# Gated heads: the value experts' columns laid out with the expert innermost

## The reference

```python
gates = sigmoid((x @ w_gate).reshape(b, n, HEADS, EXPERTS).transpose(0, 2, 1, 3))
sel = argmax(gates, axis=-1)
gm = one_hot(sel, EXPERTS) * gates
values = einsum('bhne,ehdk,bnd->bhnk', gm, value_experts, x)
sim = einsum('bhid,bhjd->bhij', q * SCALE, k)        # causal mask, then softmax
out = einsum('bhij,bhjk->bhik', attn, values)
out = einsum('bhne,ehkd,bhnk->bhnd', gm, output_experts, out)
return out.sum(axis=1)
```

## Time and profile before

| what | value |
|---|---|
| runs, us | 4002.11, 4003.85, 4009.77 (median 4003.85) |
| profiled execution, us | 4002.22 |
| its span, us | 4000.5 |
| mean granted TensorE clock | 0.958 |
| TensorE matmul busy | 3622.6 us (91%) |
| TensorE weight load busy | 3018.5 us (75%) |
| VectorE busy | 2943.7 us (74%) |
| ScalarE busy | 2167.8 us (54%) |
| stage `gated_heads` | about 2808 to 4000 us |

### The profile page before, as it was taken

One profiled execution on the slowest core, in us unless ns is written; L12 is line 12 of the kernel. 1 busy time (PEld: TensorE's weight loads), 2 busy tenths in 40 slices (PEclk: granted clock), 3 DMA queues, 4 the chain that ended last, 5 costly groups with the idle time before them and its releaser, 6 DMA issues. The chain is left out here.

```text
span 4000.5 us, 93426 instructions
## 1 busy us (share of the span) xinstructions
PE 3622.6 (91%) x28994; PEld 3018.5 (75%) x28994; DVE 2943.7 (74%) x9189; ACT 2167.8 (54%) x6661; POOL 300.2 (8%) x382
## 2 busy tenths in 40 slices
PE   6999999899999998079877879998799999999998
PEld 5888888688888887069755656666588888888887
DVE  5666666677777775556567768888888888888886
ACT  5777777677777774135344447777333333333333
POOL 0000000000000000521286000000000000000000
PEclk9999999899999997589989889999899999999999
DMA  2000000100000002422211000000200000000000
GB/s 97 0 0 0 0 0 0 47 24 10 10 10 10 16 6 101 132 94 78 71 48 31 0 19 21 16 21 16 93 14 11 13 10 13 8 10 13 10 11 9
DMA packets 56112, 109.74 MB, mean 27 GB/s; under 512 B 8368, under 2 KB 27184, under 8 KB 55728
## 3 DMA queue, kind: packets, MB, share of 16 engines
q1 hardware_dynamic: 46656, 80.72, 6.3%
q0 software_dynamic: 8464, 26.22, 2.0%
q10 hardware_dynamic: 864, 1.19, 0.1%
HBM read 72.46 MB, written 35.65 MB: 27 GB/s over the span
## 5 line engine op out<-in xcount | busy, mean ns | idle before, releaser
L639 ACT ACTIVATE c_pr<-c_sm,c_nmx 128x256 f32<-128x256 f32 x512 | 254.5, 499 | 153.6 <-DVE c_nmx L485 153.6
L127 PE MATMUL f_ps_out<-f_out_rounded,f_zgT 128*128 128x256 f32 x1024 | 310.4, 303 | 0.0
L128 PE MATMUL f_ps_out<-f_out_rest,f_zgT 128*128 128x256 f32 x1024 | 288.7, 282 | 0.0
L129 PE MATMUL f_ps_out<-f_out_rounded,f_zgT 128*128 128x256 f32 x1024 | 286.5, 280 | 0.0
L639 ACT ACTIVATE a_pr<-a_sm,a_nmx 128x128 f32<-128x128 f32 (+1 forms) x512 | 227.3, 445 | 106.0 <-DVE a_nmx L485 105.9
L485 DVE CUSTOM_DVE_ANT_0 a_sm<-a_ps_s,causal 128x128 f32<-128x128 f32 (+1 forms) x512 | 152.6, 355 | 164.2 <-PE a_ps_s L371 164.2
L2151 DVE TENSOR_REDUCE f_v<-f_gv 128x64 f32<-128x512 f32 x256 | 268.6, 1049 | 0.4
L1742 ACT ACTIVATE c_pr<-c_ps_s,c_nmx 128x256 f32<-128x256 f32 x512 | 213.8, 499 | 88.9 <-DVE c_nmx L1574 88.9
L485 DVE CUSTOM_DVE_ANT_0 c_sm<-c_ps_s,c_mask 128x256 f32<-128x256 f32 x512 | 186.8, 421 | 92.0 <-PE c_ps_s L371 90.2
L2301 ACT CAST f_zgT<-f_ps_g 128x512 fp32r<-128x512 f32 x256 | 151.3, 591 | 184.4 <-PE f_ps_g L2031 184.4
L2142 DVE TENSOR_TENSOR f_gv<-f_ps_v,f_gm_step 128x512 f32<-128x512 f32 x256 | 175.2, 684 | 98.1 <-PE f_ps_v L129 86.6
(11 more groups left out here) (377 smaller groups left out, 11442.2 us busy)
## 6 DMA issues: line engine op xcount, KB each, us to landing
f_slot_rows<-f_run POOLq DMA_DIRECT2D x1, 9216.0 KB, 34.9
f_rows<-f_slot_rows SPq DMA_DIRECT2D x72, 128.0 KB, 2.0
f_slot_out<-f_y SPq DMA_DIRECT2D x72, 128.0 KB, 1.9
c_ctx_stage<-in_ctxT SPq DMA_DIRECT2D x32, 256.0 KB, 2.8
small<-in_f_w SPq DMA_DIRECT2D x16, 512.0 KB, 3.9
x_sb<-in_x SPq DMA_DIRECT2D x8, 512.0 KB, 7.9
small<-in_c_w SPq DMA_DIRECT2D x8, 512.0 KB, 3.8
c_mask_stage<-in_mask SPq DMA_DIRECT2D x16, 256.0 KB, 3.0
```

What stands on the lines that cost most here:

```text
L127: nc.tensor.matmul(out, sh, mh, start=start, stop=False, **kw)
L128: nc.tensor.matmul(out, sh, ml, start=False, stop=False, **kw)
L129: return nc.tensor.matmul(out, sl, mh, start=False, stop=stop, **kw)
L639: last = nc.scalar.activation(pr[:, r, i, 0:n], sm[:, j, i, 0:n], ACT.Exp, bias=nmx[:, j, i:i + 1], scale=-1.0, accum_out=sums[:, r, i:i + 1])
```

## The change

The columns of `f1_val` are laid out as (channel, expert): column k*8 + e. The gating reads PSUM and writes `gv` in that order, with the eight gates broadcast along the channels, and the sum reads eight adjacent words. The sum adds the same eight terms in the same order of experts. Sizes, counts, waits and the order of the work stay.

```diff
-        gv = sb("gv", [P, 2, E, 64])
+        gv = sb("gv", [P, 2, 64, E])
...
-                nc.vector.tensor_tensor(gv[:, k % 2], ps_v[i][:].rearrange("p (e k) -> p e k", e=E),
-                                        gm_step[:, s, i, j, :].unsqueeze(2).broadcast_to([P, E, 64]), ALU.mult).then_inc(v_gated, 1)
+                nc.vector.tensor_tensor(gv[:, k % 2], ps_v[i][:].rearrange("p (k e) -> p k e", e=E),
+                                        gm_step[:, s, i, j, :].unsqueeze(1).broadcast_to([P, 64, E]), ALU.mult).then_inc(v_gated, 1)
...
-                nc.vector.tensor_reduce(v[:, s, i, 64 * j:64 * j + 64], gv[:, k % 2].rearrange("p e k -> p k e"), X,
+                nc.vector.tensor_reduce(v[:, s, i, 64 * j:64 * j + 64], gv[:, k % 2], X,
                                         ALU.add).then_inc(v_ready, 1)
...
-        "f1_val": v["L1_ffn_value_experts"].reshape(8, 8, DC, P, 64).transpose(3, 1, 2, 0, 4).reshape(P, 8, DC, 512),
+        "f1_val": v["L1_ffn_value_experts"].reshape(8, 8, DC, P, 64).transpose(3, 1, 2, 4, 0).reshape(P, 8, DC, 512),
```

## The result

The changed kernel takes 3999.33 us in the median (3993.51 to 4007.31, 20 runs), the kernel before beside it 4004.65 us (4000.03 to 4013.35, 20 runs). The ratio is 0.9985 with a 95% interval of 0.9978 to 0.9992: 6.0 us less, between 3 and 9 (the two medians lie 5.3 apart). Forecast were 3998.0 us and a gain of 5.8. The profiled execution took 3997.35 us, 4.87 less than that of before.

The account below looks back on a forecast made before the run. TensorE was taken to bound the steady part and VectorE only the first steps. Sixteen sums at 0.363 us gave 5.8 us, the gating 0: 4002.22 to 3996.4 us profiled, 1.6 more for a median of 3998.0; range 3991 to 4005.

Parts of the forecast that it names:

- The sum, 363 ns less: Expert sum L2151: 1049 to 686 ns, priced by a routed-experts row of the same shape; bounds 0 and 363.
- The estimate of 346 ns: Expert sum: saving for 512 columns by the skill's 1.73 and 1.054 ns per column; 5.5 us on the path.
- The rival that the 64 outputs cost and not the distance: Expert sum gets no faster, as each of its 64 outputs costs, not the stride: 4003.9 us; chance 0.06.
- The gating, nothing: Gating L2142: nearest row 691 ns against 684; taken as 0, bounds -0.2 to +0.2 us.
- 16 of 256 sums on the path, 5.8 us: Steps 0 to 4: sixteen sums ahead of step 4's z copy, 0.363 us each, bring that copy 5.8 us earlier.
- Step 3, where I had looked for one: VectorE's L120 in step 3: 0.1 us of room to ScalarE's rounding; gain may fall short by 0.1 to 0.2 us.
- The 17th sum gains nothing: Sum behind step 4's z copy: a VectorE 0.36 us quicker waits at L120 for ScalarE's rounding instead.
- The steady part gives nothing: From step 5 on: TensorE is full, its 17.57 us per step covers the other 239 sums, period unchanged.
- the rival by which the pauses of "issue" ahead of the scores would go: Steady steps: freed VectorE time also removes 0.37 us pauses in 59 steps, 22 us more, 3976 us; chance 0.07.
- the other side: Steady steps: denser on-chip reads slow TensorE by 0.27 us a step, 16 us in 59 steps, 4014 us; chance 0.09.
- The feed of the weights: Steps 1 to 4: rounding or transfer not ready, nothing gained from step 3 on, 3.3 us, 4000.6 us; chance 0.08.
- where the freed time would stand: Steady part: VectorE's 85.7 us wait for TensorE's values grows by about 80; its busy time falls by 93 us.

Follow-up runs that it names:

- the strides run: Changed kernel plus 22 VectorE sums and gatings in several orders behind the last step: sum 682 to 686 ns with terms 1 or 2 apart, 1011 at 64.
- early_strided: Changed kernel with the sum reading words 64 apart again in the first two batches only: ratio 0.9998 to the kernel before, stage 1172.1 us.
- steady_strided: Changed kernel with the sum reading words 64 apart from the third batch on, dense before: ratio 0.9982 to the kernel before, stage 1166.3 us.
- pad_steady: Changed kernel plus an unused tile and a 288-word reduction ahead of each of 224 sums from the third batch on: ratio 0.9971 to the kernel before.

## Why the prediction was right

**The sum, 363 ns less: measured 373** (1049 to 676). The single row of another stage had the right shape and layout and served as the price; it was 10 ns high. The estimate of 346 ns from the Trainium skill, "Vector Engine (DVE) Microarchitecture Reference", § 5.2 Measured stream behaviour on trn2, was 27 short. The rival that the 64 outputs cost and not the distance falls: the strides run has both speeds with the same 64 outputs. So the 363 that I had as the upper bound of this term was none; it was passed by 10 ns, or 16 x 0.010 = 0.2 us on the path.

**The gating, nothing: measured +3 ns**, 0.05 us on the path.

**16 of 256 sums on the path, 5.8 us: measured 5.83** from the first gating to the z copy, and early_strided shows that there is no more of it elsewhere. By the measured 0.373 the sixteen would give 6.0. The missing 0.1 us lies ahead of them, at the fourth gating of step 0, before and after:

```profile
2834.08 0.69 DVE L2142 TENSOR_TENSOR f_gv<-f_ps_v,f_gm_step 128x512 f32<-128x512 f32 x1 [0.60 <-PE f_ps_v L129]
```

```profile
2835.37 0.69 DVE L2142 TENSOR_TENSOR f_gv<-f_ps_v,f_gm_step 128x512 f32<-128x512 f32 x1 [1.06 <-PE f_ps_v L129]
```

Counted from the first gating it comes after 6.18 us instead of 6.09, because it waits for TensorE. From the fourth sum (2834.80 and 2836.10) to the z copy it is 48.89 us before and 42.96 after: 5.93 less, or 0.37 for each of the sixteen. Step 3, where I had looked for one, has none: its L120 starts at 2867.90 without a wait.

**The 17th sum gains nothing: right**, and by the mechanism named, 0.34 us of waiting for L114 ahead of L120.

**The steady part gives nothing: right.** The period is 17.57 us, and steady_strided and pad_steady show from both sides that VectorE's speed costs nothing there, within 99 us of added work. That rules out the rival by which the pauses of "issue" ahead of the scores would go: they are still 20.4 us in 55. It rules out the other side too, since denser reads would have to lengthen a step by 0.1 us, and the steps agree to 0.01.

**The feed of the weights: no new bound.** The steps from the second on lost 1.03, 1.53, 1.53 and 1.83 us (9.56, 12.11, 14.24 and 15.26 to 8.53, 10.58, 12.71 and 13.43), where four sums each would give 1.49; had the feed become the bound from step 3 on, the later steps would have kept their length.

**Mis-sized: where the freed time would stand.** I said that the wait for TensorE's values, 85.7 us, would grow by 80. The waits after the change, same view and stage as the earlier trace rows:

```profile
DVE f_gv L2142 <- PE f_ps_v L129: 109.6, 94, 3.3
DVE f_zgT L2201 <- ACT f_zgT L2301: 47.7, 96, 0.6
```

It grew by 24. ScalarE's copy of zgT, a wait of 14.5 us before, took 33 more, and the wait for the output product (f_x_sum) went from 11.4 (13 times) to 17.8 (14 times). VectorE does several kinds of work in a slot, each bound to another engine's pace, and the freed time is shared among all of these places. It made no difference to the time. Likewise VectorE's busy time fell by 86.3 us (2943.7 to 2857.4) and not by 93, though the lengths of its sums fell by 95.4: neighbouring instructions overlap by some hundredths of a us in the profile, the busy time counts that once, and where VectorE now waits between two of them there is no overlap to take off.

**What the forecast left to chance.** I gave the difference of the profiled execution from the median 1.6 us; in these runs it is 2.0. The result is 1.3 us above the forecast.

## What to carry to other kernels

A sum that reads its terms 64 words apart from the on-chip memory costs VectorE half as much again (676 to 1049 ns for 512 words; from 4 words apart on it was slow, at 2 apart it was not), but the gain of mending it is only the part that lies on the path: here 16 of 256 instructions, in the first steps. Find that part by following the engine in order of time and counting, not by the busy share, and look for the next wait behind the last one counted. If an order has to be turned somewhere, turn it on a read of PSUM, which was free here, and neither on a read nor a write of the on-chip memory; the weights needn't be touched. And a variant that adds instructions or a tile moves what stands behind them: give it a control that moves them alone.

## What the runs showed of the hardware

- VectorE's sum has two speeds for one shape: 682 to 686 ns with terms 1 or 2 words apart or in adjacent pairs, 1006 to 1068 ns with terms 4 to 64 apart. A product written 8 words apart takes 1072 for 691; one that reads PSUM 64 apart takes 691.
- 32 bytes more ahead of some of the tiles of this stage (those from `sm` on) take 0.2 us off each batch (71.63 to 71.42), with TensorE full in both.
- 32 more instructions ahead of VectorE's loop bring a pause of 2.7 us in 12 of its turns, and a ratio of 1.0061 to the kernel before, for 0.9976 without them; 16 more entries (semaphore increments) bring none.
- Beside a subtraction on GpSimd (2.34 us) a VectorE operation of 0.29 us takes 2.44, and a pair of 0.55 takes 2.10; a reduction (0.28) isn't held.
